# Splitting the trigonometry of linear attention into a front that runs a tile earlier, with its copies moved and a scaling given to VectorE

## The reference, cut to what matters

```python
def _softmax_kernel(x, R):
    n = jnp.sqrt(jnp.sum(x * x, axis=-1, keepdims=True))
    x = x / jnp.maximum(n, 1e-06)
    p = jnp.einsum('...d,ed->...e', x, R)
    feats = jnp.concatenate([jnp.sin(p), jnp.cos(p)], axis=-1)
    return feats / math.sqrt(F)
...
qp = _softmax_kernel(q, rand_matrix)
kp = _softmax_kernel(k, rand_matrix)
kv = jnp.einsum('bhsf,bhsd->bsfd', kp, v)
out = jnp.einsum('bhsf,bsfd->bhsd', qp, kv)
...
mod = (_silu(L0_c) @ L0_wmod).reshape(L0_c.shape[0], 6, 1, -1)
```

## Time and profile before

| | us |
|---|---|
| median of 2 runs | 3944.41 |
| lowest and highest run | 3838.15 and 4050.68 |
| profiled execution, device time | 3838.26 |
| span of its slowest core (core 1) | 3836.7 |
| spans of all cores | 3801.5 to 3836.7 |
| busy: PE, DVE, ACT, POOL | 2505.1, 1264.7, 517.3, 169.4 |

### The profile page before, as it was taken

One profiled execution on the slowest core, in us unless ns is written; L12 is line 12 of the kernel. 1 busy time (PEld: TensorE's weight loads), 2 busy tenths in 40 slices (PEclk: granted clock), 3 DMA queues, 4 the chain that ended last, 5 costly groups with the idle time before them and its releaser, 6 DMA issues.

```text
span 3836.7 us, 31886 instructions; the slowest of 8 cores (3801.5 to 3836.7 us)
## 1 busy us (share of the span) xinstructions
PE 2505.1 (65%) x10824; PEld 1082.9 (28%) x10824; DVE 1264.7 (33%) x2208; ACT 517.3 (13%) x507; POOL 169.4 (4%) x294
## 2 busy tenths in 40 slices
PE   3349822124972232673499589986899589976886
PEld 1124311112431111231244234432344234432332
DVE  0456255454623433446322122211222122211203
ACT  0111132333113323102100000000000000000000
POOL 0000000000001011000000000000000000000000
PEclk8559955556985566785599789998999789998997
DMA  9513101002353555310243964558543964458547
GB/s 164 107 55 66 27 24 28 17 25 47 66 97 69 98 93 137 67 23 1 61 84 54 207 226 77 93 110 225 161 86 66 210 219 81 93 117 235 156 82 265
DMA packets 84936, 395.06 MB, mean 103 GB/s; under 512 B 7184, under 2 KB 7440, under 8 KB 75312
## 3 DMA queue, kind: packets, MB, share of 16 engines
q0 software_dynamic: 41536, 208.26, 31.3%
q1 hardware_dynamic: 33696, 146.98, 11.1%
q10 hardware_dynamic: 9552, 37.80, 2.7%
HBM read 538.26 MB, written 46.20 MB: 152 GB/s over the span
## 4 chain that ended last, share of the span: by engine, by line
PE 52%; DMA 20%; DVE 12%; issue 8%; ACT 7%; DVEq 0%; ACTq 0%; POOL 0%; POOLq 0%; SPq 0%
PE pb L965 23%; PE pb L573 9%; PE pb L1041 8%; DMA AW<-w2scr 4%; DMA AW<-w2i 4%; DMA w2scr<-AW 3%; PE pb L839 3%; DMA AW<-w1i 3%; DMA AW<-wmod 3%; ACT AMS L734 2%; PE pb L421 2%; PE pb L539 2%; DVE AHT L544 1%; PE pb L509 1%; DVE AMS L1053 1%
## 5 line engine op out<-in xcount | busy, mean ns | idle before, releaser
L965 PE MATMUL pb<-AHT,AW 128*128 128x512 bf16 x4608 | 1010.2, 382 | 61.6 <-DMA AW<-w1i 50.8
L1041 PE MATMUL pb<-AW,AOT 128*128 128x512 bf16 x2304 | 589.0, 422 | 280.1 <-DMA AW<-w2i 149.9
L965 PEld LDWEIGHTS pb<-AHT,AW 128*128 128x128 bf16 x4608 | 452.0, 98 | 619.5 <-issue 88.6
L1041 PEld LDWEIGHTS pb<-AW,AOT 128*128 128x128 bf16 x2304 | 240.9, 106 | 628.2 <-issue 417.8
L573 PE MATMUL pb<-AW,AHT 128*128 128x512 bf16 x1536 | 352.9, 383 | 0.0
L1053 DVE TENSOR_TENSOR AMS<-pb,AMS 128x2048 f32<-128x2048 f32 x40 | 91.7, 2291 | 713.2 <-PE pb L1041 709.8
L989 ACT ACTIVATE AMS<-AMS 128x1024 f32<-128x1024 f32 x64 | 67.7, 1057 | 1433.2 <-DVE AMS L986 1433.1
L539 PE MATMUL pb<-identf,AX 128*128 128x128 f32 x256 | 99.6, 445 | 202.5 <-ACT AX L500 151.6
L745 PE MATMUL pb<-AMS 128*128 128x128 bf16 x128 | 34.3, 268 | 298.8 <-ACT AMS L734 298.8
L991 DVE TENSOR_TENSOR AMS<-pb,AMS 128x1024 f32<-128x1024 f32 x64 | 78.4, 1224 | 370.5 <-PE pb L965 370.5
L573 PEld LDWEIGHTS pb<-AW,AHT 128*128 128x128 bf16 x1536 | 143.6, 98 | 183.6 <-issue 27.5
(11 more groups left out here) (132 smaller groups left out, 1677.9 us busy)
## 6 DMA issues: line engine op xcount, KB each, us to landing
AW<-w2scr SPq DMA_DIRECT2D x54, 2048.0 KB, 9.1
AW<-wmod POOLq DMA_DIRECT2D x24, 2048.0 KB, 18.5
w2scr<-AW ACTq DMA_DIRECT2D x18, 2048.0 KB
AW<-w1i POOLq DMA_DIRECT2D x32, 1024.0 KB, 9.0
AW<-w3i POOLq DMA_DIRECT2D x32, 1024.0 KB, 8.9
AW<-w2i POOLq DMA_DIRECT2D x16, 2048.0 KB, 22.0
AX<-xin SPq DMA_DIRECT2D x16, 1024.0 KB, 4.9
AW<-wqt POOLq DMA_DIRECT2D x4, 2048.0 KB, 17.7
```

Source lines behind the costliest of these rows:

```text
L965: ins = tt.matmul(pu[:, th * 512:(th + 1) * 512], slot(sl)[:, ic * 128:(ic + 1) * 128], ahtb[:, ic * 1024 + th * 512: ic * 1024 + (th + 1) ...
L1041: ins = tt.matmul(pw[:, ob * 512:(ob + 1) * 512], hebuf[:, hc * 1024 + tau * 128: hc * 1024 + tau * 128 + 128], slot(ws)[:, ob * 512:(ob + ...
```

## The change

`emit_mid_B` is split. The new `emit_mid_F(sh, t)` (the front) holds L690 to L707 and the eight DMAs into `v16`; `emit_mid_B` keeps the placing and the products. The front of tile t is recorded right after the back of tile t - 1. The four operations L734 go from ACT (a scaled identity) to DVE (a multiplication by 0.5, one source). Four scratch tiles change places in memory, so that the front no longer shares bytes with the transposed q and k.

```diff
-        wabs = amsf[:, 2688:3712]
-        kfb = amsf[:, 0:1024]
-        wfr = amsf[:, 1024:2048]
-        a2f = amsf[:, 1024:2048]
+        wfr = amsf[:, 2688:3712]
+        a2f = amsf[:, 2688:3712]
+        kfb = amsf[:, 1024:2048]
+        wabs = amsf[:, 1024:2048]
...
-        c2b = amsb[:, 0:1024]
+        c2b = amsb[:, 15104:16128]
...
-        def emit_mid_B(sh, t):
+        def emit_mid_F(sh, t):
...
             sch.op("scalar", lambda s: s.activation(
                 c2b[:], a2f[:], AF.Sin, bias=cpi[:, 4:5]),
-                reads=["a2f", "cpi"], writes=W(ar_ms, "c2b", 0, 2048))
+                reads=["a2f", "cpi"], writes=W(ar_ms, "c2b", 30208, 32256))
+            vbk = f"vb{sh}_{t}"
+            for g in range(8):
+                sch.dma("gpsimd", lambda gg, t=t, g=g: gg.dma_start(
+                    v16[:, g * 128:(g + 1) * 128], vb_t(t)[g * 16:(g + 1) * 16, :]),
+                    reads=[vbk],
+                    writes=W(ar_ms, f"v16_{g}", 8192 + g * 256, 8192 + (g + 1) * 256))
+
+        def emit_mid_B(sh, t):
...
-                    cph = cpi[64 * half:64 * half + 64, 5:6]
-                    sch.op("scalar", lambda s, c2h=c2h, dcos=dcos, cph=cph: s.activation(
-                        dcos, c2h, AF.Identity, scale=cph),
-                        reads=["c2b", "cpi"], writes=[dk])
-            for g in range(8):
-                sch.dma("gpsimd", lambda gg, t=t, g=g: gg.dma_start(
-                    v16[:, g * 128:(g + 1) * 128], vb_t(t)[g * 16:(g + 1) * 16, :]),
-                    reads=[vbk],
-                    writes=W(ar_ms, f"v16_{g}", 8192 + g * 256, 8192 + (g + 1) * 256))
+                    sch.op("vector", lambda v, c2h=c2h, dcos=dcos: v.tensor_scalar(
+                        dcos, c2h, 0.5, None, ALU.mult),
+                        reads=["c2b"], writes=[dk])
...
             emit_mid_A(0, t)
             if t:
                 emit_mid_B(0, t - 1)
+            emit_mid_F(0, t)
             emit_ln1_tile(1, t, True, None, lnxsA,
...
             emit_mid_A(1, t)
             if t:
                 emit_mid_B(1, t - 1)
+            emit_mid_F(1, t)
             emit_mod_jb(8 + 2 * t)
             emit_mod_jb(9 + 2 * t)
```

More of the change, by code:

```diff
@@ L680, in emit_mid_A @@
                        writes=W(tra, pk2, pcq * 4, pcq * 4 + 2048))
-        def emit_mid_B(sh, t):
+        def emit_mid_F(sh, t):
             par = t % 2
-            vbk = f"vb{sh}_{t}"
             trb = pb0 if par == 0 else pb1
             trn = "pb0" if par == 0 else "pb1"
-            tra = ar_p0 if par == 0 else ar_p1
             upq, upkk = "prq" + trn, "prk" + trn
@@ L692, in emit_mid_B @@
             sch.op("scalar", lambda s: s.copy(kfb[:], ti32[:]),
-                   reads=["ti32"], writes=W(ar_ms, "kfb", 0, 4096))
+                   reads=["ti32"], writes=W(ar_ms, "kfb", 4096, 8192))
             sch.op("vector", lambda v, up=up: v.tensor_sub(wfr[:], up, kfb[:]),
-                   reads=[upq, upkk, "kfb"], writes=W(ar_ms, "wfr", 4096, 8192))
+                   reads=[upq, upkk, "kfb"], writes=W(ar_ms, "wfr", 10752, 14848))
             sch.op("scalar", lambda s: s.activation(s1b[:], wfr[:], AF.Sin,
@@ L699, in emit_mid_B @@
             sch.op("scalar", lambda s: s.activation(wabs[:], wfr[:], AF.Abs),
-                   reads=["wfr"], writes=W(ar_ms, "wabs", 10752, 14848))
+                   reads=["wfr"], writes=W(ar_ms, "wabs", 4096, 8192))
             sch.op("scalar", lambda s: s.activation(
@@ L705, in emit_mid_B @@
                 a2f[:], wabs[:], AF.Abs, scale=cpi[:, 3:4], bias=cpi[:, 1:2]),
-                reads=["wabs", "cpi"], writes=W(ar_ms, "a2f", 4096, 8192))
+                reads=["wabs", "cpi"], writes=W(ar_ms, "a2f", 10752, 14848))
             sch.op("scalar", lambda s: s.activation(
                 c2b[:], a2f[:], AF.Sin, bias=cpi[:, 4:5]),
-                reads=["a2f", "cpi"], writes=W(ar_ms, "c2b", 0, 2048))
+                reads=["a2f", "cpi"], writes=W(ar_ms, "c2b", 30208, 32256))
[6 more added lines that the diff above has]
+        def emit_mid_B(sh, t):
+            par = t % 2
+            trb = pb0 if par == 0 else pb1
+            trn = "pb0" if par == 0 else "pb1"
+            tra = ar_p0 if par == 0 else ar_p1
             for half in range(2):
```

## The result

The changed kernel took 3880.3 us (median of 11 runs), the kernel before 3847.5 us on the same chips (10 runs). The ratio is 1.0094, with a 95% interval of 1.0065 to 1.0123. So the change costs about 36 us where +75 us was forecast: the sign is right, the size is half. The change is within the 2% that were given 0.40, less than the 0.56 for slower. Some executions of every kernel run in a slower state of the chip; the medians are over all executions and the ratios over the others alone, so a ratio needn't be the quotient of two medians.

A forecast was written before the change was run, and what follows sets the result against it. The prediction took a chain of dependent steps across engines to bound the tile loops. It summed -6 us (sh = 0) and +81 (sh = 1) to +75: 3838 + 75 = 3913 us, range 3875 to 3962.

The forecast's parts named there:

- What bounds the kernel: Tile loops of both token halves: no engine is full; a chain of dependent steps passing between engines sets their length.
- Part 1: Order in the tile loops: the front follows the previous tile's back, replacing 19.05 us there, but Square stands behind it.
- sum of sh = 0: First-half tile loop: -1.6 us per middle tile, seven times -11; first tile +12.7, last tile -7.7; together -6 us.
- Part 2: Placing in the back: eight DVE operations in a row, 0.42 us per query operation, 1.27 per new key operation, 9.2 together.
- B: Loads exposed as forecast, but each new key operation in the placing costs 2.42 to 2.55 us: 3950 to 3954; chance 0.30.
- C: Loads exposed as forecast, but each new key operation in the placing costs 0.41 us: 3885 us; chance 0.12.
- Part 3: POOL's queue in sh = 1: v16 copies delay both wmod loads; tiles 1 to 6 +67, sh = 1 +81 us.
- T to the next tile: In sh = 1, from a tile's first modulation product to the next tile: 39.1 us, where it was near 17.8.
- A to T: In sh = 1, from the start of part A to the first modulation product: 29.0 us, where it was 38.73.
- Rival D: In sh = 1 the wmod loads stay hidden because the copies find their buffer free earlier: 3758 us; chance 0.04.
- rival E: In sh = 1 the pair of wmod loads shares the engines evenly and lands together: +60, 3973 us; chance 0.04.
- Tile 7: Last tile of sh = 1, to the first rearranging copy: 95.1 us where it was 86.2, or +9.

The follow-up runs named there:

- a_vback: a_own with the eight copies into v16 recorded in the back again, before the products; 3788.7 us, ratio 0.9755 to the kernel before.
- a_two: a_own with a second buffer for v16, used in turn, the copies keeping their place in the queue; 3744.7 us, ratio 0.9742 to the kernel before.
- a_split: a_vback with the front's sines and absolute values recorded after the layer norm in sh = 0; 3683.9 us, ratio 0.9574 to the kernel before.
- b_own: The kernel before, with each instruction's waits recorded with the engine's own semaphore first; 3820.1 us, ratio 0.9919 to the kernel before.
- a_own: The changed kernel, with each instruction's waits recorded with the engine's own semaphore first; 3899.4 us, ratio 1.0107 to the kernel before.
- b_pe: The kernel before, with the own semaphore waited for first on TensorE alone and last on all other engines; 3831.0 us, ratio 0.9948.
- b_scale: b_own with only the scaling L734 moved from ACT to DVE; 3817.6 us, ratio 0.9917 to the kernel before.
- b_vonly: b_own with only the eight copies into v16 moved, recorded right after the rest of the previous tile; 3944.7 us, ratio 1.0237 to the kernel before.

## Why the prediction was right and wrong, step by step

**What bounds the kernel.** Right: latencies on the chain set the tile loops. DVE and PE are far from full in the tile loops of both kernels, and taking one wait out of the chain (a_vback, a_two) or one piece from it (a_split) moved the time about as the sums of the earlier trace rows said.

**Part 1 and the sum of sh = 0.** Right with equal orders of waits: a middle tile goes from 57.4 us (b_own) to 55.9 (a_own), -1.5 against -1.6; the stretch from tile 1 to the q product -17.9 against -18.6; the start +10.4 against +12.7. Against b_pe they are -19.1 and +12.2. In the given pair the two stretches are 8.7 and 6.6 us below the forecast, since their pairs of transposes are 0.1 us shorter, eight to a tile.

**Part 2, the placing.** Right: 1.29 us for a key operation (1.27 taken), 2.43 for the two-source one beside it, on the same target. Rivals B and C are out. The query operation was 0.29, not 0.42; the rounded pauses between dependent operations took that back (9.5 us for the back, from 558.51 to 568.00, against 9.3). That the scaling by itself would be worth nothing in the old order stood in no sentence of mine; b_scale shows it.

The page "Advanced Engine Details and Errata" of the Trainium skill ("Memory Cachelines") asks for two hits per 16-byte line. The measured 2.43 us for two sources agree with a penalty for one hit per line. By the code, the first and the second half of the new operation's elements fall into the same lines, which would make two hits if one of each half is written at a time; no run varied the step, so that reason for the 1.29 us is argued and not shown. "VectorE: DVE Perf Modes" of the Trainium skill ("What auto-detection actually checks") allows the one-source operation a second port, and the 1.29 us agree with it.

**Part 3, the queue.** Right, and shown from both sides: the copies' move alone costs 3.2% (b_vonly), undoing it gives 3.5% (a_vback), and freeing the copies from their wait in the same place gives as much (a_two). T to the next tile was taken as 39.1 us; the row gives 1322.76 less about 1284.3, some 38.5. The second load landed after 26.7 us, 27.3 were taken. A to T, 29.0 forecast, is about 29.0. Over tiles 1 to 6 the sum of 406 us was 9.5 too high: the second load landed after 26.4 us in the mean, the two issues were 0.55 us apart where 1.05 were taken, and the second product took 5.7 us in the mean where 5.8 were taken. The reason given for the 5.8, a longer idle time before it, is not borne out by the pair shown above: the product after 17.75 us of idle time took 5.00 us at a mean granted clock of 0.72, the one after 2.66 us took 6.42 at 0.56. The same tiles are 4 us shorter in b_pe than in the kernel before, so the change itself costs +61.8 there against +67. Rival D is out by the issue at 1285.47, rival E by the landings of 16.5 and 26.7 us. Tile 7 gained less than the +9 forecast (+6.8): its pair landed after 18.8 and 34.0 us, where 37.4 were assumed for the second.

**The total.** This is the step that failed: "-6 + 81 = +75". Each of its two terms compares the kernel before with the changed one as if all instructions outside the diff kept their times; the order of the waits was put at nothing, without a reason. But TensorE waits for its own semaphore last in the kernel before and first in the changed one, and each pair of transposes is 0.106 us shorter from the opening on. On the kernel before, this order alone is worth -20 us by the ratio of b_pe (uncertainty 13 us), and -28 us between the spans of the profiled executions. With one order for both kernels the change costs +56 us (against b_pe), +72 (own first) or +55 (own last), with uncertainties of 17, 30 and 20 us; in the given pair it costs 0.94%, +36 us, which is +56 less 20. So the missing term is about half of the 39 us between forecast and measurement by the ratios, and 28 of 38 us by the spans. The rest is in the two terms themselves: by the spans they are 10 us too high together, half of it in tiles 1 to 6 of sh = 1 (part 3).

What is shown: the order of waits moves this kernel by 55 us, it makes the hops of 1.22 and 1.11 us, the two given builds differ in it, and with nearly the same order the stretches come out within 5.2 us of their forecasts. What stays open: no second build of the given files with the old code was made, so how often the orders fall this way is not known. The last stretch of the first table, -10 us, is -2.0 against b_pe and holds only stages that the change doesn't touch; between cores of one and the same execution it varies from 2149 us (core 2 before) to 2167 us (core 1 before).

## What to carry to other kernels

Before a DMA is moved in an issuing queue, read what it waits for: a copy whose buffer comes free late takes every load behind it along, and a 2 MB load that used to be a tile early is then a whole landing late. A piece of work that is moved to an earlier iteration is hidden only if its engines have nothing behind it that the chain wants; here the early front gained 1.5 us a tile in the first half, and some 8 us more once its sines were recorded behind the layer norm's own ACT work.

If a scheduler sorts by anything that isn't fixed, such as addresses, two builds of the same text can be two kernels. Fix the order first, then compare; and look in both traces at a stage that the change doesn't touch, and at the order of the wait instructions themselves.

## What the runs showed of the hardware

- The order in which an instruction's waits are recorded matters. A wait on TensorE that is already satisfied still took 0.106 us when it stood behind the one that came late. With the late one at the end, a hop from VectorE to TensorE and back is that much shorter (pair of transposes 1.11 us against 1.22), and the whole kernel 1.4% faster when all engines do so. TensorE's waits carry most of it.
- A VectorE operation with one source, 512 elements of 2 bytes written with a step of 16 bytes, takes 1.29 us; one with two sources onto the same target 2.42 us. With runs of 16 elements as the target they take 0.29 and 0.42 us.
- Two casting loads of 2 MB, issued together by POOL, landed after 16.5 and 26.7 us; in the seven pairs of the changed kernel's second tile loop the first took 16.2 to 18.8 us and the second 25.4 to 34.0.
